# Softmax sums from one joined operand of the first group, formed one unit later

## What is computed

```python
scores = clip(einsum(q, k), -80, 80), causal mask
weights = softmax(scores / sqrt(192))
attn = einsum(weights, v)
out = attn @ W_O.T
```

## Time and profile before

| | |
|---|---|
| time, median of 3 runs | 1307.34 us (1306.8 to 1307.97) |
| the profiled execution | 1306.28 us, of which span 1304.4 us |
| busy, share of the span | PE 98%, PEld 80%, DVE 55%, ACT 50%, POOL 48% |
| the chain that ended last | PE 92%, POOL 2%, DVE 2%, issue 1%, DMA 1%, ACT 1% |
| matmuls | 6233 |
| granted TensorE clock | full in all 40 slices |

### The profile page before, as it was taken

One profiled execution on the slowest core, in us unless ns is written; L12 is line 12 of the kernel. 1 busy time (PEld: TensorE's weight loads), 2 busy tenths in 40 slices (PEclk: granted clock), 3 DMA queues, 4 the chain that ended last, 5 costly groups with the idle time before them and its releaser, 6 DMA issues.

```text
span 1304.4 us, 20533 instructions
## 1 busy us (share of the span) xinstructions
PE 1279.4 (98%) x6233; PEld 1047.0 (80%) x6233; DVE 722.1 (55%) x1349; ACT 648.6 (50%) x1163; POOL 626.0 (48%) x535
## 2 busy tenths in 40 slices
PE   4999999999999999999999999999999999999998
PEld 3788898888888888888887688887888888887886
DVE  6472255223222222222224788888888888888777
ACT  6411133222222222222225677777777777777775
POOL 5125566995060003300001577677667777676543
PEclk9999999999999999999999999999999999999999
DMA  9226564664251113311112243322243223323012
GB/s 299 66 98 230 212 221 122 191 183 151 66 154 58 60 55 105 109 62 58 58 49 86 75 97 66 63 47 60 48 79 50 51 54 66 63 37 67 18 50 98
DMA packets 82168, 123.34 MB, mean 95 GB/s; under 512 B 20177, under 2 KB 28497, under 8 KB 82065
## 3 DMA queue, kind: packets, MB, share of 16 engines
q1 hardware_dynamic: 48912, 56.43, 15.5%
q0 software_dynamic: 11312, 27.23, 9.6%
q10 hardware_dynamic: 21840, 38.36, 9.1%
HBM read 74.41 MB, written 39.05 MB: 87 GB/s over the span
## 4 chain that ended last, share of the span: by engine, by line
PE 92%; POOL 2%; DVE 2%; issue 1%; DMA 1%; ACT 1%; SPq 0%; ACTq 0%; POOLq 0%; DVEq 0%
PE bank L49 86%; PE bank L1505 2%; PE bank L1446 2%; PE bank L1588 1%; DMA rot_sin<-sum_b 0%; DMA rows_a<-in_x 0%; POOL sum_b L614 0%; POOL rot_sin L583 0%; POOL slots L493 0%; POOL sum_b L611 0%; POOL rstd L488 0%; POOL rot L588 0%; POOL sum_b L616 0%; SPq L435 0%; DVE stats L945 0%
## 5 line engine op out<-in xcount | busy, mean ns | idle before, releaser
L49 PE MATMUL bank<-store_b,store_a 128*128 128x512 f32 (+1 forms) x1536 | 319.1, 359 | 3.2 <-issue 1.2
L49 PE MATMUL bank<-slots,x_turned 128*128 x1296 | 317.6, 394 | 0.3 <-DVE x_turned L969 0.3
L49 PEld LDWEIGHTS bank<-store_b,store_a 128*128 128x128 f32 x1536 | 256.1, 189 | 60.3 <-issue 8.7
L49 PEld LDWEIGHTS bank<-slots,x_turned 128*128 128x128 f32 x1296 | 239.2, 188 | 48.1 <-issue 0.7
L991 DVE TENSOR_TENSOR hid_t<-bank,hid_t 128x512 fp32r<-128x512 f32 x70 | 48.4, 691 | 342.2 <-ACT hid_t L682 342.2
L49 PE MATMUL bank<-slots,hid_t 128*128 (+1 forms) x840 | 208.4, 397 | 0.0
L49 PE MATMUL bank<-store_b 128*128 128x512 f32 x768 | 180.1, 390 | 0.1
L49 PEld LDWEIGHTS bank<-slots,hid_t 128*128 128x128 f32 x840 | 153.7, 188 | 30.9 <-DVE hid_t L991 0.2
L49 PEld LDWEIGHTS bank<-store_b 128*128 128x128 f32 x768 | 143.8, 188 | 31.1 <-issue 0.9
L1342 DVE TENSOR_TENSOR store_b<-p_store,store_b 128x512 fp32r<-128x512 f32 x128 | 137.0, 1073 | 26.9 <-ACT store_b L863 26.8
L676 ACT ACTIVATE hidden<-bank 128x512 f32<-128x512 f32 x70 | 41.8, 597 | 208.3 <-PE bank L49 208.3
(11 more groups left out here) (200 smaller groups left out, 1767.7 us busy)
## 6 DMA issues: line engine op xcount, KB each, us to landing
staging<-in_w SPq DMA_DIRECT2D x56, 256.0 KB, 2.8
sorted_y<-y_store ACTq DMA_DIRECT2D x54, 256.0 KB, 2.0
rows<-sorted_x ACTq DMA_DIRECT2D x51, 260.0 KB, 2.7
rot_sin<-sum_b SPq DMA_DIRECT2D x128, 64.0 KB, 2.0
staging<-in_wg SPq DMA_DIRECT2D x28, 256.0 KB, 2.8
y_store<-in_x ACTq DMA_DIRECT2D x16, 256.0 KB, 3.4
shared_y<-y_store ACTq DMA_DIRECT2D x16, 256.0 KB, 2.2
raw<-in_wot SPq DMA_DIRECT2D x16, 256.0 KB, 2.8
```

Source lines behind the costliest of these rows:

```text
L49: made = pe.matmul(out, a, b, start=first and n == 0, stop=last and n == len(pairs) - 1, skip_group_check=onto)
```

## The change

GpSimd adds the first quarter-pair of group 2 to the second-query half of group 0's exponents, in place in `p_store` (L617 of the changed kernel), as soon as their exponents are there, ahead of `sine(u+1)`. ScalarE rounds the result to `sum_a_hi` (L937), behind the last `round_high` and ahead of `query(u+1)`; GpSimd subtracts to `sum_a_lo` (L637), behind `sum_b_lo` and ahead of the gathers. `sums` then has two products for the first operand and two for `sum_b`, all 512 wide: four in place of six. `sums(u)` is no longer issued at the end of `attend(u)` but in unit u + 1, behind `rotate`, ahead of groups 2 to 4 of the scores; in the last unit it keeps its place. ScalarE's `sums_row(u-1)` moves accordingly from the end of its unit to a place behind the second `round_high`; SyncE's transfer is a function `send_divisors(u-1)`, issued right behind the swaps (ahead of the loads of weights); VectorE's `invert(u-1)` moves behind `take_low` of groups 1 and 2. The writers of `p_hi` and `p_lo` wait for `o_done` in place of `dens_done`, and group 0's slot in `p_store` is now held until `first_low`. The diff leaves out the semaphores' names and the edits told here in words.

```diff
@@ -243,6 +243,8 @@
         sin_t = tile(ctx, "sin_t", [P, SEQ], side="right")
         sum_b = tile(ctx, "sum_b", [P, 2, H2], side="right")
         rot_raw = sum_b[:].rearrange("p h t -> p (h t)")
+        sum_a_hi = tile(ctx, "sum_a_hi", [P, BANK], F32R, side="right")
+        sum_a_lo = tile(ctx, "sum_a_lo", [P, BANK], F32R, side="right")
 
         sems(*(f"x_in{n}" for n in range(NT)), "scattered0", "scattered1", "padded0", "padded1", *(f"staged{n}" for n in range(NS)), *(f"row_in{n}" for n in range(3)),
              *(f"y_sent{n}" for n in range(2)), "gate_in", "consts_in", "zeros_in",
...
@@ -312,19 +314,18 @@
                 ring.take("scores", u, g)
                 if g == 1 and u + 1 < NU:
                     ring.take("rotate", u + 1)
+                if g == 1 and u:
+                    ring.take("sums", u - 1)
             if u + 1 < NU:
                 ring.take("query", u + 1, 0)
                 ring.take("query", u + 1, 1)
             if u:
                 for tt in range(TB):
                     ring.take("output", u - 1, tt)
-            if u:
-                ring.take("sums", u)
             for h in heads_of(u):
                 ring.take("head", p + 1, h, 0)
                 ring.take("head", p + 1, h, 1)
-            if not u:
-                ring.take("sums", u)
+        ring.take("sums", NU - 1)
         for tt in range(TB):
             ring.take("output", NU - 1, tt)
 
...
@@ -356,9 +357,9 @@
                 dve.wait_ge(on["y_done"], NBK)
                 return
             v, f = divmod(n, NG)
-            dve.wait_ge(on["sum_step"], 3 * v + 3)
+            dve.wait_ge(on["sum_step"], 4 * v + 4)
             if f == 0:
-                dve.wait_ge(on["p_low0"], v + 1)
+                dve.wait_ge(on["first_low"], v + 1)
             else:
                 dve.wait_ge(on["p_low"], (NG - 1) * v + f)
 
...
@@ -600,26 +606,36 @@
             for u in range(NU):
                 pool.wait_ge(on["p_high"], NG * u + 1)
                 if u:
-                    pool.wait_ge(on["dens_done"], u)
+                    pool.wait_ge(on["o_done"], 2 * u)
                 pool.tensor_tensor(p_lo[0], prob(u, 0), p_hi[0].bitcast(F32), ALU.subtract).then_inc(on["p_low0"], 1)
 
                 w = [prob(u, g).rearrange("p (h t) -> p h t", h=2) for g in range(NG)]
+                w1_q1 = prob(u, 2)[:, 0:2 * P].rearrange("p (h t) -> p h t", h=2)
                 w3_q3 = prob(u, 2)[:, 2 * P:4 * P].rearrange("p (h t) -> p h t", h=2)
+                pool.wait_ge(on["p_low0"], u + 1)
+                pool.wait_ge(on["exps_done"], NG * u + 3)
+                pool.tensor_tensor(w[0][:, :, P:2 * P], w[0][:, :, P:2 * P], w1_q1, ALU.add).then_inc(
+                    on["sum_step"], 1)
                 if u + 1 < NU:
                     sine(u + 1)
                 pool.wait_ge(on["exps_done"], NG * u + 4)
                 pool.tensor_tensor(sum_b[:], w[1], w[3], ALU.add).then_inc(on["sum_step"], 1)
                 pool.wait_ge(on["exps_done"], NG * u + 5)
-                pool.wait_ge(on["sum_step"], 3 * u + 1)
+                pool.wait_ge(on["sum_step"], 4 * u + 2)
                 pool.tensor_tensor(sum_b[:], sum_b[:], w[4], ALU.add).then_inc(on["sum_step"], 1)
-                pool.wait_ge(on["sum_step"], 3 * u + 2)
+                pool.wait_ge(on["sum_step"], 4 * u + 3)
                 pool.tensor_tensor(sum_b[:, :, P:2 * P], sum_b[:, :, P:2 * P], w3_q3, ALU.add).then_inc(
                     on["sum_step"], 1)
                 if u + 1 < NU:
                     rotate(u + 1)
                 pool.wait_ge(on["sums_high"], u + 1)
+                if u:
+                    pool.wait_ge(on["dens_done"], u)
                 pool.tensor_tensor(sum_b_lo, sum_b[:], sum_b_hi.bitcast(F32), ALU.subtract).then_inc(
                     on["sums_low"], 1)
+                pool.wait_ge(on["first_high"], u + 1)
+                pool.tensor_tensor(sum_a_lo[:], prob(u, 0), sum_a_hi[:].bitcast(F32), ALU.subtract).then_inc(
+                    on["first_low"], 1)
                 if u >= 2 and u - 2 < NT // 2 * TOP_K:
                     n, b = divmod(u - 2, NB)
                     pool.wait_ge(on["out_added"], TB * (u - 1))
...
@@ -902,6 +918,8 @@
                 round_high(u, 0)
                 exponents(u, 2)
                 round_high(u, 1)
+                if u:
+                    sums_row(u - 1)
                 exponents(u, 3)
                 exponents(u, 4)
                 round_high(u, 2)
...
@@ -913,10 +931,14 @@
                     rescale(u - 1, 2)
                     rescale(u - 1, 3)
                 round_high(u, 4)
+                act.wait_ge(on["sum_step"], 4 * u + 1)
+                if u:
+                    act.wait_ge(on["dens_done"], u)
+                act.activation(sum_a_hi[:], prob(u, 0), ACT.Copy).then_inc(on["first_high"], 1)
                 if u + 1 < NU:
                     query(u + 1, 0)
                     query(u + 1, 1)
-                act.wait_ge(on["sum_step"], 3 * u + 3)
+                act.wait_ge(on["sum_step"], 4 * u + 4)
                 act.activation(sum_b_hi, sum_b[:], ACT.Copy).then_inc(on["sums_high"], 1)
                 if u + 1 < NU:
                     rotate_high(u + 1)
...
@@ -930,8 +952,6 @@
                     act.wait_ge(on["o_done"], 2 * u + n + 1)
                     act.activation(o_split[:, 0, n], o_banks[n].rearrange("p (h t) -> p h t", h=2),
                                    ACT.Copy).then_inc(on["o_high"], 1)
-                if u < NU - 1:
-                    sums_row(u)
                 for h in heads_of(u):
                     head_weights(p + 1, h, 0)
                     head_weights(p + 1, h, 1)
...
@@ -1392,10 +1412,10 @@
                     rotate(u + 1)
                 clip(u, 3)
                 clip(u, 4)
-                if u:
-                    invert(u - 1)
                 take_low(u, 1)
                 take_low(u, 2)
+                if u:
+                    invert(u - 1)
                 take_low(u, 3)
                 if u:
                     output(u - 1, 0)
...
@@ -1688,10 +1708,8 @@
                 ring_bank_free(pe, "sums", u)
                 pe.wait_ge(on["unit_rounded"], 1)
                 row = ring.bank("sums", u)[0:2, :]
-                second_half = row.rearrange("p (h t) -> p h t", h=2)[:, :, P:2 * P]
-                product(pe, row, [(unit_r[:, 0, :], s[0]) for s in (p_hi, p_lo)], last=False)
-                product(pe, second_half, [(unit_r[:, 0, :], s[2][:, 0:2 * P].rearrange("p (h t) -> p h t", h=2))
-                                          for s in (p_hi, p_lo)], first=False, last=False)
+                pe.wait_ge(on["first_low"], u + 1)
+                product(pe, row, [(unit_r[:, 0, :], sum_a_hi[:]), (unit_r[:, 0, :], sum_a_lo[:])], last=False)
                 pe.wait_ge(on["sums_low"], u + 1)
                 product(pe, row.rearrange("p (h t) -> p h t", h=2),
                         [(unit_r[:, 1, :], sum_b_hi), (unit_r[:, 1, :], sum_b_lo)], first=False).then_inc(
...
@@ -1720,8 +1738,6 @@
                         made = product(pe, dst, split3(ckv[:, 0, t, :], ckv[:, 1, t, :], hi, lo), first=j == 0,
                                        last=j == len(steps) - 1)
                     made.then_inc(on["o_done"], 1)
-                if u < NU - 1:
-                    sums(u)
 
             head_weights(0, 0, 1)
             turn_hidden(NBK - 1)
...
@@ -1733,6 +1749,8 @@
                 scores(u, (0, 1))
                 if u + 1 < NU:
                     rotate(u + 1)
+                if u:
+                    sums(u - 1)
                 scores(u, (2, 3, 4))
                 if u + 1 < NU:
                     query(u + 1, 0)
```

More of the change, by code:

```diff
@@ L262, in program @@
              "q_done", "q_high", "q_low", "scores_done", "exps_done", "clipped", "p_high", "p_low0", "p_low",
-             "sum_step", "o_done", "o_high", "o_low", "sums_high", "sums_low", "dens_done", "rows_made", "inverted",
+             "sum_step", "o_done", "o_high", "o_low", "first_high", "first_low", "sums_high", "sums_low", "dens_done", "rows_made", "inverted",
              "ratio_made", "part_done", "rescaled", "out_done", "out_added")
@@ L436, in swap_halves, with send_divisors @@
                     sp.dma_start(rot_sin[b:c, :], rot_raw[a:b, :]).then_inc(on[f"rot_swapped{u % 2}"], 16)
+            def send_divisors(u):
+                sp.wait_ge(on["rows_made"], u + 1)
+                if u >= 2:
+                    sp.wait_ge(on["ratio_made"], u - 1)
+                for s in range(2):
+                    sp.dma_start(sum_store[:, u % 2, s].rearrange("p h t -> p (h t)"),
+                                 divisor_rows[s:s + 1, :].rearrange("o (p c) -> o p c", p=P)).then_inc(
+                        on[f"divisor_sent{u % 2}"], 16)
             rotary_weights(0)
@@ L463, in sync_program @@
                     head_weights(p + 1, h)
-                sp.wait_ge(on["rows_made"], u + 1)
```

(15 more changed lines are left out.)

1 line of the change is left out of this document (added).

## The result

| | before | after |
|---|---|---|
| median of 4 runs | 1307.3 us (1306.8 to 1307.97) | 1396.9 us (1396.15 to 1398.13) |
| ratio | | 1.0689 (95%: 1.0676 to 1.0701) |
| profiled execution, span | 1306.28, 1304.4 us | 1396.15, 1394.3 us |
| matmuls | 6233 | 6169 |

The change makes the kernel 6.9% slower: 89.6 us between the medians, 89.9 between the spans. The page of the changed kernel, busy time of each engine, and from its fourth part the shares of the chain that ended last.

The account below looks back on a forecast made before the run. It took TensorE and an equally long ring of waits to bound the kernel in balance; 18 plain units at 3.4 us, 12 with head products at 2.35 and 1.6 for the last gave 91.0 on 1306.28: 1397 us, range 1333 to 1435.

Parts of the forecast that it names:

- ScalarE done with L779: ScalarE from first rescale through second query (4.53 us), new rounding (0.55) and following instructions (1.95): done at 18.6 us.
- two loops in balance: Before the change, TensorE's matmuls (17.90 us a plain unit) and a ring of waits through the other engines (17.89) equally long.
- the whole gain on offer: TensorE's sums lose one full product width, 0.23 us a unit: 7.4 us in all if nothing else moved.
- Rival 4: Faster: the divisors' way is covered after all and TensorE keeps its 0.23 us a unit: 1299 us; chance 0.06.
- The transfer: Divisors' DMAs on SyncE, right behind the swaps, land 2.0 us after issue (4.1 the upper end), at 10.4 us.
- rival 3: More turns on take_low and ratio, or divisors needing 4.1 us: 22.5 us a unit, 1433 us; chance 0.12.
- the ring: Waits through all other engines, from the rotated query's low part back to itself: plain unit 17.9 to 21.3 us.
- The ratio's turn: VectorE's ratio takes turns with GpSimd's instructions: 0.8 us, half a long instruction (bounds 0 and 2.0); rescale at 11.6.
- L637's turn: GpSimd's new subtraction takes its turn before or between VectorE's last two ring instructions: 1.25 us (bounds 0 and 1.3).
- Units with head products: Twelve units, 18.94 us by TensorE alone before, also become 21.3: 2.35 us more each, 28.2 in all.
- The tail: Last unit keeps its sums in attend, behind one more GpSimd instruction (1.30) and ScalarE copy (0.55), less 0.23: 1.6 us.
- L617 at nothing: GpSimd's new addition ahead of the sine costs nothing: at most 1.3 us, covered by 2.11 of waiting for swaps.

Follow-up runs that it names:

- Experiment 10: Kernel before without the two 256-wide products of its sums (half the divisors lack one block of keys), nothing added or moved: 1306.39 us, ratio 0.9991.
- Experiment 1: Changed kernel with GpSimd's two subtractions in the other order, sum_a_lo (L637) ahead of sum_b_lo (L634): 1368.84 us, ratio 1.0469.
- 6: Changed kernel with VectorE's ratio made by four multiplications by a per-partition scalar instead of one of two SBUF tensors: 1385.57 us, ratio 1.0596.
- the lateness alone: Kernel before with its six products one unit late, row, transfer and inversion placed as in the change, no joined operand: 1380.83 us, ratio 1.0571.
- the join alone: Changed kernel's joined operand, but sums, row, transfer and inversion in the places of the kernel before, L637's subtraction first: 1340.38 us, ratio 1.0253.
- experiment 3: Changed kernel with sums_row ahead of group 2's exponents and invert ahead of both take_low: 1370.07 us, ratio 1.0477.

## Why the prediction was right

The time was forecast at 1397 us and came out at 1396.9. Agreement to that figure is luck. The terms for the 30 units between the first and the last come to 61.2 + 28.2 = 89.4 us, and the 31 intervals measured gave 84.0, 5.4 less; the tail was forecast at 1.6 and measured 5.4, 3.8 more; 0.5 lay ahead of the loop. So the span grew by 89.9 where 91.0 was forecast, and the median run lay 0.75 above the profiled one. The mechanism held step by step, in the unit shown, from the end of L1275 (the forecast is for a plain unit):

| step | forecast | measured |
|---|---|---|
| exponents of group 2 start | 5.52 | 5.53 |
| row of divisors done | 7.80 | 7.65 |
| divisors landed | 10.4 | 10.3 (chain of waits: 2.04 us of transfer) |
| `rescale` starts | 11.6 | 11.35 |
| ScalarE done with L779 | 18.6 | 17.96 |
| L1275 ends | 21.3 | 20.69 |

- **The bound.** Right: two loops in balance. Experiment 10 shows it more sharply than I used it: I called 7.4 us "the whole gain on offer" and gave a faster result 0.06 in which TensorE keeps it; with nothing else changed that gain is at most 0.19%, by the interval. Rival 4's 1299 us had no ground even with the divisors in time.
- **The transfer.** The choice of 2.0 over 4.1 us held: the median of `sum_store` from issue to landing is 2.1 in the changed kernel. In rival 3 a transfer of 4.1 us would have added 2.1 to the 21.3, 23.4 us, and not the 22.5 that it was given. What the forecast had not is the units of 22.1 us; they hide that the ordinary ring was 0.6 too long. In seven intervals, every fourth, the divisors land at 11.0 to 11.5 us of the ring in place of 10.3. In the trace each of these seven, and no other, has a packet of 16 KB in the queue called instruction, between the issue of the divisors and their landing, which took 0.96 to 1.35 us. (The second interval, 22.0 us too, has none; there the row itself is 1.3 us late.) The interval ahead of the unit shown, 22.09 us long, has one between 1054 and 1058 us, here in the DMA view of that stretch, with two lines of the timeline behind it:

```profile
q8 instruction: 1, 0.02, 1.6%
...
1058.40 1.26 POOL L625 TENSOR_TENSOR sum_b<-sum_b,p_store 128x512 f32<-128x512 f32 x1
1058.49 1.19 DVE L1398 TENSOR_TENSOR ratio<-inv_store,sum_store 128x4 f32<-128x4 f32 x1
```

  The ratio has missed the end of L622 and ends with the next addition, L625: 0.9 us of lateness costs 1.4. In six intervals this is some 8.4 of the 84.0 us; in the seventh the ratio slipped between the two additions (0.16 us), and it took 20.83. The late swap of experiment 10 has such a packet beside it too. That the packet is what delays the transfer was not tested.
- **The ratio's turn.** The mechanism was right; I priced it as half a long instruction, 0.8 in the mean. It is in fact tied to the end of L622, or of L625 where it comes late: 0.70 where 0.16 would do in the unit shown (0.54), 924 ns in the median (0.76). Taken out alone it gives 11.3 us / 31 = 0.36 a unit: part of what it costs is waited for elsewhere anyway.
- **ScalarE.** 6.61 us from `rescale` to the end of L779 against 7.03: the new rounding takes 0.52 where 0.55 was forecast, L942, L778 and L779 1.80 where it was 1.95, and the rest 4.29 where it was 4.53.
- **L637's turn.** Taken from L1342 at 1.25, measured 0.83 on L1274 (1.51 against 0.68). The other 0.52 between L779's end and L1274's start is L1286, VectorE's own queue, which I had not named. The sum of both (2.72 with L1275) was near the forecast's 2.63. Experiment 1 puts the turn at 0.9 a unit. The Trainium skill (SBUF — State Buffer, "Who interferes with whom") states that a VectorE instruction with two SBUF inputs contends with a GpSimd instruction that reads SBUF, and one with at most one SBUF input, outside modes that it names, does not. Experiments 1 (two inputs: L1274 took 1520 ns in the median, and 735 once L637 stood elsewhere) and 6 (one input, 217 ns at most) agree.
- **Units with head products.** Forecast at 2.35 over before, measured 20.92 against 18.90: 2.02. Plain ones: 3.4 forecast, 21.34 against 18.07: 3.27, and the first interval, for which there was no term, grew by 0.99. (In the changed kernel the products of a unit run ahead of its last L1275, in the kernel before behind its last L1255; each mean is of the 12 or 18 intervals as they fall in its own trace.) That plain units are the longer ones is the work of the late transfers; without these both kinds take the same time, as said.
- **The tail.** The term that was mis-sized: 1.6 forecast, 5.4 measured. I had counted only ScalarE's and GpSimd's extra step ahead of the sums; the last unit also has the wait at `rescale`, which I had counted for the units between only. In the timeline of the last unit TensorE stands 2.35 us there and 0.63 for L637. The granted clock fell as well: it was full up to 1376.7, through TensorE's wait that ended at 1375.24, and 0.50 (1.2 GHz) from 1376.7 to 1380.1. The window above and the same stretch of the kernel before, below, divide the loss: TensorE stood idle for 7.2 us against 3.5, 3.8 more, and was busy for 24.1 against 22.3, 1.7 more for one matmul less, as much as 3.4 us at half the clock would cost.

```profile
1278.60:1304.40 25.80, 22.34 (x102) 16.71 (x100) 18.04 (x26) 14.55 (x24) 6.58 (x5) 0.99 0.23 83
...
1375.24 4.57 PE L49 MATMUL bank<-store_b 128*128 128x512 f32 x12 [2.35 <-ACT bank L898]
...
1381.67 0.40 PE L49 MATMUL bank<-sum_a_hi,unit_r 128*2 128x512 f32 x1 [0.63 <-POOL sum_a_lo L637]
```

- **L617 at nothing.** Right: 0.74 us, and the sine still waits 0.80 for the swaps behind it.
- **Parts of the loss.** The forecast gave the lateness and the turns as terms that add up. They don't: the lateness alone costs 73.5 us and the join alone 33, together more than the 89.6; taking L637's turn out gives 28 back, the ratio's 11. The traces show two ways round (through L1275 and through TensorE's own wait at `rescale`); that each part shows its price only while its way is the longer is my reading of this, and no run separates them.

What stayed open: whether the packets of instructions delay the divisors, and how the 89.6 us divide among steps that overlap.

## What to carry over

In a kernel whose engines wait for each other in a ring, follow that ring from one instruction back to itself before removing work from the busiest engine: if it is as long as the busy engine's own work, the removed work is worth next to nothing (here 0.19% at most), and a wait added to it is paid in each round, unless a second way round is as long. When a result is to be used later, its whole way must be placed anew, queues included (here: the row behind exponents, its transfer behind four swaps, the inversion behind two subtractions). And look at what an added GpSimd instruction runs beside: the last VectorE step of the ring, if it reads two operands from SBUF, waits for it (0.83 us a unit here).

## What was not expected of the hardware

- An operation of 128 x 4 elements took up to 1254 ns (924 in the median) beside GpSimd, since it ended only with GpSimd's instruction (30 of 32 times), and 161 in a gap between two; the same values from four operations with a per-partition scalar took 0.58 us in all, undisturbed.
- Turns alternate: once GpSimd has waited for VectorE its own instruction stretches as well (L622 1.73 us, 1.28 in experiment 3), so both engines are slower than alone.
- Two DMA issues held ScalarE for 1.23 us, as long as they hold SyncE (1.17 to 1.18); on a compute engine that is time of the ring.
- The granted clock was full (2.4 GHz) in all slices before; with TensorE waiting for about 10% of the time its mean was 0.99 from 820 to 1250 us and 0.94 in the last 31.3 us, where it cost about 1.7 us.
- The divisors' transfers of 2 KB landed 0.7 to 1.2 us later than usual in just the seven units in which a 16 KB packet of the instruction queue was in flight beside them.
